# Recurrence of a four-layer graph network: product and sum as one scan, gate biases by matmul

## Chip, cores and metric

One core of a Trainium2 chip runs the whole program. The metric is the device time of one execution in microseconds. Below, PE is the matrix engine TensorE, ACT is ScalarE, DVE is VectorE, POOL is GpSimd and SP is SyncE.

## Reference

The model has four layers, each a graph step and a feed-forward step, over 64 sequences of 128 positions and 128 features, in float32. The change lies in the feed-forward step of the first layer, a recurrence over the 128 positions (B = 64 sequences side by side, H = 128 features on the partitions):

```python
xi = xt @ U_i + b_i
xg = xt @ U_c + b_c
xo = xt @ U_o + b_o
def step(carry, xs):
    h, c = carry
    ...
    i_t = jax.nn.sigmoid(xi_t + h @ V_i)
    g_t = jnp.tanh(xg_t + h @ V_c)
    o_t = jax.nn.sigmoid(xo_t + h @ V_o)
    c_new = h * c + i_t * g_t
    h_new = o_t * jnp.tanh(c_new)
    return ((h_new, c_new), h_new)
```

Step t + 1 needs the h of step t, so the 128 steps can't overlap.

## The kernel before

The program is a row of blocks; between two of them all engines meet at a barrier. The block of the recurrence comes second (lines 385 to 468). It has three programs that run side by side and meet through semaphores, and a POOL part that only clears two tiles at its start (lines 397 and 398).

**PE.** Time is cut into 16 turns of 8 steps (STEPS = 8). A turn uses three of six PSUM banks, one for each gate, and the banks alternate between turns by `par`. For each gate, `inputs` (line 407) writes U times the inputs of a whole turn into its bank in two halves of 256 columns; it is called six times ahead of the first step, and then once in each of the first six steps of a turn for the turn that follows. Each step waits for h (line 412), then adds V times h to its own 64 columns of the three banks, in the order i, c, o (line 417). A float32 matmul is two passes in the trace, each with a weight load, so a step has six passes of 64 columns there. Behind them in PE's order come the `inputs` of the step, in steps 0 to 63 a one-column matmul for row sums that the second layer needs (line 423), and fillers of 256 columns that write a bank that nobody reads (line 425). There are two fillers in a step with `inputs` and three in one without; in steps 0 to 63 there is one fewer.

**ACT.** Each step has three activations from PSUM to the tile `gates`, with the gate's bias (one value on each partition, a column of EXP) as bias operand (line 440): sigmoid for i, tanh for c, sigmoid for o. Then it waits for the cell and takes its tanh (line 443).

**DVE.** Each step has four products or sums of 128 x 64: h times the old cell into `hc` (line 454), gate i times gate c into `ig` (line 458), `hc` plus `ig` into the cell (line 461), and gate o times tanh of the cell, the new h, into `AUX` (line 464). The waits of an instruction are written ahead of it, one to a line. Line 458 has first the wait for gate c (`s.gt`) and then the one for gate i (`s.it`). Line 461 has first the one for `hc`, then the one for `ig`. Line 464 has first the one for gate o, then the one for tanh of the cell.

The biases are loaded by SP in the first block, behind its input transfers, one value on each partition (line 242). EXP is a work tile that holds U, V and biases here; its columns 4096 to 4479 hold weights of the second layer.

## Time and profile before

| | us |
|---|---|
| median of 3 runs | 1961.46 |
| the runs | 1950.76, 1961.46, 1961.59 |
| span of the profiled execution | 1867.1 |
| median less span | 94.4 |
| the steps of the recurrence within the span | from about 115 to 406 |

The profile gives the span of its execution, from the first to the last instruction, and no device time of its own for it; the 94.4 us are what an execution has around that span, if it took as long as the median run. The profile has the busy time of each engine, the start and length of each instruction, what ended an engine's idle time, and the clock that TensorE was granted as a share of its full speed.

### The profile page before, as it was taken

The numbers are of one execution on the slowest core, as the hardware profiler recorded it, in microseconds if no ns is written. First come the engines' busy times: TensorE is split into PE (matmuls) and PEld (weight loads), VectorE is DVE, ScalarE is ACT, GpSimd is POOL, SyncE is SP. The second block draws the span as 40 slices with busy tenths as digits, with TensorE's granted clock in tenths as the row PEclk, the third lists the DMA queues.
The fourth block names the chain that finished last, engine by engine and source line by source line (L and its number), as shares of the span: only waits on it lengthen the run. The fifth ranks groups of instructions, "written<-read, shape, count | busy, mean of one in ns | idle before, by whom it ended". The sixth has DMA issues, their size and how long they took to land. (4 is left out here: it accounts for less than half of the span.)

```text
span 1867.1 us, 43356 instructions
## 1 busy us (share of the span) xinstructions
PE 1627.8 (87%) x13366; PEld 1314.2 (70%) x13366; DVE 1095.9 (59%) x4199; ACT 998.9 (53%) x3116; POOL 786.7 (42%) x1358
## 2 busy tenths in 40 slices
PE   7978899988859987999998888879999888884995
PEld 5756677767759985788887566679999845553542
DVE  7933433348737777699998755523333377763552
ACT  5854444446636656666665433246666534441663
POOL 6710000014426666111111677745565434554675
PEclk9989999999969999899999799989999989995998
DMA  3200000010014420000000511122222253105331
GB/s 114 84 1 1 1 1 1 1 27 1 1 36 134 123 80 1 2 3 2 2 3 3 156 47 48 62 62 70 72 71 72 56 150 86 58 24 88 100 86 35
DMA packets 125926, 91.76 MB, mean 49 GB/s; under 512 B 23591, under 2 KB 116554, under 8 KB 125701
## 3 DMA queue, kind: packets, MB, share of 16 engines
q1 hardware_dynamic: 109110, 61.89, 12.6%
q0 software_dynamic: 13568, 25.90, 4.3%
q10 hardware_dynamic: 3024, 1.21, 0.4%
q8 instruction: 114, 1.87, 0.4%
q14 instruction: 110, 0.90, 0.2%
HBM read 57.71 MB, written 33.30 MB: 49 GB/s over the span
## 5 line engine op out<-in xcount | busy, mean ns | idle before, releaser
L1361 ACT ACTIVATE FEAT<-BANKS,FEAT 128x128 f32<-128x128 f32 x544 | 155.5, 368 | 82.1 <-PE BANKS L1314 82.1
L1206 POOL DMA_INDIRECT scratch_made<-FEAT x136 | 144.9, 1065 | 122.6 <-DVE FEAT L1500 119.8
L1061 ACT ACTIVATE EXP<-BANKS,NEGMAX 128x128 f32<-128x128 f32 x512 | 139.4, 383 | 59.5 <-DVE NEGMAX L1073 59.5
L440 ACT ACTIVATE gates<-BANKS,EXP 128x64 f32<-128x64 f32 x384 | 97.4, 314 | 112.6 <-PE BANKS L417 112.6
L1314 PE MATMUL BANKS<-FEAT 128*128 128x128 f32 x1088 | 145.5, 277 | 0.0
L1323 PE MATMUL BANKS<-AUX,FEAT 128*128 x1088 | 144.5, 276 | 0.4 <-ACT FEAT L1361 0.4
L417 PEld LDWEIGHTS BANKS<-AUX,EXP 128*128 128x128 f32 x768 | 95.4, 191 | 69.7 <-DVE AUX L464 69.6
L1198 POOL DMA_INDIRECT scratch_sent<-FEAT,POS x128 | 125.1, 977 | 38.3 <-issue 37.5
L990 POOL COPY EXP<-AUX 128x32 f32<-128x32 f32 x256 | 42.5, 211 | 217.8 <-PE BANKS L1036 217.8
L1314 PEld LDWEIGHTS BANKS<-FEAT 128*128 128x128 f32 x1088 | 133.9, 194 | 0.0
L1323 PEld LDWEIGHTS BANKS<-AUX,FEAT 128*128 128x128 f32 x1088 | 133.2, 193 | 0.6 <-issue 0.6
L503 POOL TENSOR_SCALAR NEG<-MV 128x4 f32<-128x4 f32 x16 | 3.7, 229 | 303.1 <-DVE MV L176 303.1
L417 PE MATMUL BANKS<-AUX,EXP 128*128 128x64 f32 x768 | 112.8, 283 | 18.6 <-DVE AUX L464 16.6
L425 PE MATMUL BANKS<-FEAT,ident 128*128 128x256 f32 x460 | 126.7, 393 | 0.0
L1500 DVE TENSOR_TENSOR FEAT<-BANKS,B2BC 128x128 f32<-128x128 f32 x136 | 39.5, 290 | 133.1 <-PE BANKS L1323 133.1
L1624 POOL DMA_INDIRECT out_x<-FEAT x96 | 94.1, 980 | 52.1 <-issue 28.4
L846 ACT ACTIVATE WF<-BANKS,BT 128x128 f32<-128x128 f32 x256 | 73.2, 368 | 41.1 <-PE BANKS L820 41.1
L458 DVE TENSOR_TENSOR ig<-gates 128x64 f32<-128x64 f32 x128 | 28.7, 224 | 111.7 <-ACT gates L440 111.7
L1073 DVE TENSOR_REDUCE NEGMAX<-BANKS 128x4 f32<-128x512 f32 x128 | 82.6, 686 | 18.5 <-PE BANKS L1012 18.2
L425 PEld LDWEIGHTS BANKS<-FEAT,ident 128*128 128x128 f32 x460 | 80.8, 191 | 7.4
L1493 DVE COPY FEAT<-AUX 128x512 f32 x136 | 58.1, 427 | 47.1 <-issue 47.0
L1082 DVE SCALAR_TENSOR_TENSOR EXP<-AT,BANKS 128x512 f32<-128x512 f32 x128 | 81.8, 679 | 0.5 <-PE BANKS L1023 0.5
(367 smaller groups left out, 4196.0 us busy)
## 6 DMA issues: line engine op xcount, KB each, us to landing
EXP<-in_L_ffn_W SPq DMA_DIRECT2D x128, 128.0 KB, 2.1
FEAT<-scratch_sent SPq DMA_DIRECT2D x136, 64.5 KB
EXP<-scratch_made SPq DMA_DIRECT2D x32, 256.0 KB, 3.4
FEAT<-scratch_sent SPq DMA_DIRECT2D x96, 65.5 KB, 1.9
X<-in_x SPq DMA_DIRECT2D x16, 256.0 KB, 2.9
STAGE<-in_adj SPq DMA_DIRECT2D x16, 256.0 KB, 3.3
scratch_sent<-NONE SPq DMA_DIRECT2D x48, 65.5 KB, 3.3
scratch_sent<-FEAT,POS POOLq DMA_INDIRECT x192, 2.3
```

The costliest lines, as they stand in the source:

```text
L417: pe.matmul(PS[2 * gate_at + par][:, u * B:(u + 1) * B], wr["V" + gate], cols(HS, j, STEPS * B, u * B, B), start=False, stop=True, skip_gr ...
L425: pe.matmul(PS[7][:, 0:half], ident[:], cols(FEAT, j, STEPS * B, 0, half), start=True, stop=True)
L440: act.activation(gates[:, at, sp_, :], PS[2 * at + par][:, u * B:(u + 1) * B], f, bias=wr["b" + gate]).then_inc(done, 1)
L1061: last = act.activation(tile(EXS[:, par], 4 * k + n), tile(PS[j], c), ACT.Exp, bias=NEGMAX[:, par, 4 * k + n:4 * k + n + 1])
L1073: v.tensor_reduce(NEGMAX[:, par, 4 * k:4 * k + 4].rearrange("p (j c) -> p j c", j=2), BANKS[:, 2 * k:2 * k + 2, 0:NC * T].rearrange("p j ( ...
L1082: v.scalar_tensor_tensor(PTA[:, par, 4 * k * T:4 * (k + 1) * T].rearrange("p (n t) -> p n t", n=4), adj, ADJ_EPS, PS[4 + k].rearrange("p ( ...
L1198: pool.indirect_dma_start(out=sent2, out_offset=bass.IndirectOffsetOnAxis(ap=POS[:, n, b:b + 1], axis=0), in_=OUTBOX[:, i % R_SEND, n, k, ...
L1206: pool.indirect_dma_start(out=made2, out_offset=bass.IndirectOffsetOnAxis(ap=XI_I[:, t % R_IN, H:ROW2], axis=0), in_=YO[:, t % R_OUT, :], ...
L1314: last = pe.matmul(tile(PS[2 + t % 2], c), W1R[:, t % R_W, c * P:(c + 1) * P], XTI[:, t % 3, :], start=True, stop=True)
L1323: last = pe.matmul(PS[4 + t % 2][:, 0:H], tile(HR[:, t % R_H], c), W2_2.rearrange("p c d -> p (c d)")[:, bass.ds(e * F2 + c * H, H)], star ...
L1361: last = act.activation(tile(HR[:, t % R_H], c), tile(PS[2 + t % 2], c), ACT.Gelu, bias=BT[:, c, t:t + 1])
L1624: pool.indirect_dma_start(out=out_rows, out_offset=bass.IndirectOffsetOnAxis(ap=XI3_I[:, t % R3, H + 2:ROW3], axis=0), in_=YO3[:, t % R3, ...
```

## The change

DVE's product `ig` and its sum become one scan. Gate i and gate c are written by ACT into every second element of two tiles of 64 pairs: `by` holds (0, i) and `plus` holds (g, h times c). The scan computes state = by * state + plus along the 128 elements of a partition: at the first element of a pair the state becomes g, at the second i * g + h * c, the new cell. The zeros of `by` are written once by POOL. The scan has three waits ahead of it, in the order `hc`, gate i, gate c.

The activations of the gates lose their bias operand. The biases are loaded as rows of 128 values on partition 0 and added in PSUM by a matmul with one row of contraction: the bias row is the stationary operand, a row of ones, 256 columns wide, the moving one. There is one with each `inputs`, which makes 6 ahead of the first step and 90 within the steps; a step with `inputs` has one filler fewer (1 in steps 64 to 127, 0 in steps 0 to 63).

```diff
--- before.py
+++ after.py
@@ -224,7 +224,7 @@
         wr = {}
         for at, gate in enumerate("cio"):
             wr["U" + gate], wr["V" + gate] = (tile(EXP, 2 * at + k) for k in range(2))
-            wr["b" + gate] = EXP[:, 6 * H + at:6 * H + at + 1]
+            wr["b" + gate] = EXP[0:1, 4608 + at * H:4608 + (at + 1) * H]
         wtop, wbot = EXP[:, 4096:4096 + H], EXP[:, 4096 + H:4096 + 2 * H]
         b1rows = EXP[:, 4096 + 2 * H:4096 + 3 * H]
         with nc.Block() as block:
@@ -239,7 +239,7 @@
                 for gate in "cio":
                     sp.dma_start(wr["U" + gate], a["L0_ffn_U_" + gate]).then_inc(s.later, 16)
                     sp.dma_start(wr["V" + gate], a["L0_ffn_V_" + gate]).then_inc(s.later, 16)
-                    sp.dma_start(wr["b" + gate], column(a["L0_ffn_b_" + gate])).then_inc(s.later, 16)
+                    sp.dma_start(wr["b" + gate], a["L0_ffn_b_" + gate].rearrange("(o h) -> o h", o=1)).then_inc(s.later, 16)
                 sp.dma_start(wtop, a["L1_gnn_weight"][0:H, :]).then_inc(s.later, 16)
                 sp.dma_start(wbot, a["L1_gnn_weight"][H:2 * H, :]).then_inc(s.later, 16)
                 sp.dma_start(b1rows, a["L1_gnn_bias"].partition_broadcast(P)).then_inc(s.later, 16)
@@ -382,12 +382,12 @@
                 unrolled(NG, [(2, hT), (3, back), (2, project), (0, adjacency), (4, xT), (2, conv)])
 
         layer()
-        s = sems("rnn", "zero x_even x_odd g i o gt it ot hc ig c ct h")
+        s = sems("rnn", "zero x_even x_odd g i o gt it ot hc c ct h")
         HS = AUX
-        cell = lb("cell", [P, 2, B])
-        hc = lb("hc", [P, 2, B])
-        ig = lb("ig", [P, 2, B])
-        gates = lb("gates", [P, 3, 2, B])
+        by = lb("by", [P, 2, B, 2])
+        plus = lb("plus", [P, 2, B, 2])
+        made = lb("made", [P, 2, B, 2])
+        gate_o = lb("gate_o", [P, 2, B])
         tanhc = lb("tanhc", [P, 2, B])
         NT = T // STEPS
         ROWSUM = PS[6][:, 0:B]
@@ -395,7 +395,8 @@
             @block.gpsimd
             def _(pool):
                 pool.memset(HS[:, 0:B], 0.0).then_inc(s.zero, 1)
-                pool.memset(cell[:, 1, :], 0.0).then_inc(s.zero, 1)
+                pool.memset(made[:, 1], 0.0).then_inc(s.zero, 1)
+                pool.memset(by[:], 0.0).then_inc(s.zero, 1)
 
             @block.tensor
             def _(pe):
@@ -407,12 +408,15 @@
                     pe.matmul(PS[2 * gate_at + par][:, part * half:(part + 1) * half], wr["U" + gate],
                               cols(FEAT, j, STEPS * B, part * half, half), start=(part == 0), stop=False,
                               skip_group_check=True)
+                    pe.matmul(PS[2 * gate_at + par][:, part * half:(part + 1) * half].rearrange("p (r h) -> p r h", r=2),
+                              wr["b" + gate], ones[0:1, :].unsqueeze(1).to_broadcast([1, 2, half // 2]), start=False, stop=False,
+                              skip_group_check=True)
 
                 def turn(j, par, prefetch):
 
                     for u in range(STEPS):
                         step = j * STEPS + u
-                        pe.wait_ge(s.h if step else s.zero, step if step else 2)
+                        pe.wait_ge(s.h if step else s.zero, step if step else 3)
                         for gate_at, (gate, sem) in enumerate(zip("ico", (s.i, s.g, s.o))):
                             pe.matmul(PS[2 * gate_at + par][:, u * B:(u + 1) * B], wr["V" + gate],
                                       cols(HS, j, STEPS * B, u * B, B), start=False, stop=True,
@@ -421,7 +425,7 @@
                             inputs(j + 1, 1 - par, u // 2, u % 2)
                         if step < B:
                             pe.matmul(ROWSUM[:, step:step + 1], AT[:, step * T:(step + 1) * T], ones[:, 0:1], start=True, stop=True)
-                        for _ in range((2 if prefetch and u < 6 else 3) - (step < B)):
+                        for _ in range((1 if prefetch and u < 6 else 3) - (step < B)):
                             pe.matmul(PS[7][:, 0:half], ident[:], cols(FEAT, j, STEPS * B, 0, half), start=True, stop=True)
                 for gate_at in range(3):
                     for part in range(2):
@@ -434,13 +438,14 @@
                 def turn(j, par):
                     for u in range(STEPS):
                         step, sp_ = j * STEPS + u, u % 2
-                        for at, (gate, made, done, f) in enumerate((("i", s.i, s.it, ACT.Sigmoid), ("c", s.g, s.gt, ACT.Tanh),
-                                                                    ("o", s.o, s.ot, ACT.Sigmoid))):
-                            act.wait_ge(made, step + 1)
-                            act.activation(gates[:, at, sp_, :], PS[2 * at + par][:, u * B:(u + 1) * B], f,
-                                           bias=wr["b" + gate]).then_inc(done, 1)
+                        for at, (gate, ready, done, f, into) in enumerate((
+                                ("i", s.i, s.it, ACT.Sigmoid, by[:, sp_, :, 1]), ("c", s.g, s.gt, ACT.Tanh, plus[:, sp_, :, 0]),
+                                ("o", s.o, s.ot, ACT.Sigmoid, gate_o[:, sp_, :]))):
+                            act.wait_ge(ready, step + 1)
+                            act.activation(into, PS[2 * at + par][:, u * B:(u + 1) * B], f).then_inc(done, 1)
                         act.wait_ge(s.c, step + 1)
-                        act.activation(tanhc[:, sp_, :], cell[:, sp_, :], ACT.Tanh).then_inc(s.ct, 1)
+                        act.activation(tanhc[:, sp_, :], made[:, sp_, :, 1], ACT.Tanh).then_inc(s.ct, 1)
+                act.wait_ge(s.zero, 3)
                 for j in range(NT):
                     turn(j, j % 2)
 
@@ -451,19 +456,18 @@
                         step, q = j * STEPS + u, u % 2
                         if step:
                             v.wait_ge(s.h, step)
-                        v.tensor_tensor(hc[:, q, :], cols(HS, j, STEPS * B, u * B, B), cell[:, 1 - q, :],
+                        v.tensor_tensor(plus[:, q, :, 1], cols(HS, j, STEPS * B, u * B, B), made[:, 1 - q, :, 1],
                                         ALU.mult).then_inc(s.hc, 1)
+                        v.wait_ge(s.hc, step + 1)
+                        v.wait_ge(s.it, step + 1)
                         v.wait_ge(s.gt, step + 1)
-                        v.wait_ge(s.it, step + 1)
-                        v.tensor_tensor(ig[:, q, :], gates[:, 0, q, :], gates[:, 1, q, :], ALU.mult).then_inc(s.ig, 1)
-                        v.wait_ge(s.hc, step + 1)
-                        v.wait_ge(s.ig, step + 1)
-                        v.tensor_tensor(cell[:, q, :], hc[:, q, :], ig[:, q, :], ALU.add).then_inc(s.c, 1)
+                        v.tensor_tensor_scan(made[:, q].rearrange("p b k -> p (b k)"), by[:, q].rearrange("p b k -> p (b k)"),
+                                             plus[:, q].rearrange("p b k -> p (b k)"), 0.0, ALU.mult, ALU.add).then_inc(s.c, 1)
                         v.wait_ge(s.ot, step + 1)
                         v.wait_ge(s.ct, step + 1)
-                        v.tensor_tensor(cols(HS, j, STEPS * B, (u + 1) * B, B), gates[:, 2, q, :], tanhc[:, q, :],
+                        v.tensor_tensor(cols(HS, j, STEPS * B, (u + 1) * B, B), gate_o[:, q, :], tanhc[:, q, :],
                                         ALU.mult).then_inc(s.h, 1)
-                v.wait_ge(s.zero, 2)
+                v.wait_ge(s.zero, 3)
                 for j in range(NT):
                     turn(j, j % 2)
 
```

## Rows read from the trace of the kernel before

**Rows 1.** The page: span, and the chain that ended last, by engine.

```profile
span 1867.1 us, 43356 instructions
...
PE 9%; POOL 4%; issue 3%; ACT 1%; DMA 1%; ACTq 1%; DVE 1%; SPq 0%; POOLq 0%; DVEq 0%
```

**Rows 2.** Busy time by stretch: us, engines, granted clock, DMA share, GB/s.

```profile
110.00:115.30 5.30, 4.57 (x12) 3.74 (x13) 0.22 (x1) 1.28 (x1) 0.24 (x2) 0.54 0.01 3
...
115.30:406.30 291.00, 272.37 (x1538) 211.13 (x1536) 114.73 (x511) 130.19 (x512) 0.00 (x0) 1.00 0.00 1
```

**Rows 3.** Instructions in time, step 38: start us, us, engine, line [idle before <-releaser].

```profile
201.46 0.74 PEld L417 LDWEIGHTS BANKS<-AUX,EXP 128*128 128x128 f32 x6 [0.64 <-DVE AUX L464]
201.46 0.88 PE L417 MATMUL BANKS<-AUX,EXP 128*128 128x64 f32 x6 [0.24 <-DVE AUX L464]
201.93 0.76 ACT L440 ACTIVATE gates<-BANKS,EXP 128x64 f32<-128x64 f32 x3 [0.85 <-PE BANKS L417]
...
202.50 0.22 DVE L458 TENSOR_TENSOR ig<-gates 128x64 f32<-128x64 f32 x1 [0.84 <-ACT gates L440]
202.83 0.23 DVE L461 TENSOR_TENSOR cell<-hc,ig 128x64 f32<-128x64 f32 x1
203.09 0.26 ACT L443 ACTIVATE tanhc<-cell 128x64 f32<-128x64 f32 x1 [0.40 <-DVE cell L461]
203.45 0.22 DVE L464 TENSOR_TENSOR AUX<-gates,tanhc 128x64 f32<-128x64 f32 x1 [0.39 <-ACT tanhc L443]
...
203.72 0.74 PEld L417 LDWEIGHTS BANKS<-AUX,EXP 128*128 128x128 f32 x6 [0.64 <-DVE AUX L464]
```

**Rows 4.** Instructions in time, ACT at 202.25 to 202.30: gate c of that step.

```profile
202.15 0.31 ACT L440 ACTIVATE gates<-BANKS,EXP 128x64 f32<-128x64 f32 x1
```

**Rows 5.** Line 464 by its own view: ns min/median/max, first and last start us.

```profile
L464 DVE TENSOR_TENSOR AUX<-gates,tanhc x128: 224/225/227, 117.3 to 406.1; 128x64 f32<-128x64 f32 x128
```

**Rows 6.** ACT instructions by line and shape: busy us, mean ns | idle before.

```profile
L440 ACT ACTIVATE gates<-BANKS,EXP 128x64 f32<-128x64 f32 x384 | 97.4, 314 | 112.6 <-PE BANKS L417 112.6
...
L443 ACT ACTIVATE tanhc<-cell 128x64 f32<-128x64 f32 x128 | 32.8, 256 | 51.3 <-DVE cell L461 51.3
...
L334 ACT COPY FEAT<-BANKS 128x512 f32<-128x512 f32 x16 | 16.9, 1054 | 2.5 <-PE BANKS L195 2.5
L313 ACT ACTIVATE WB<-BANKS,w_be,w_g 128x512 f32<-128x512 f32 x16 | 12.3, 772 | 0.3 <-PE BANKS L195 0.3
L308 ACT ACTIVATE WD<-BANKS,w_b 128x512 f32<-128x512 f32 x16 | 11.0, 688 | 11.8 <-PE BANKS L368 11.8
...
L330 ACT COPY AT<-BANKS 128x512 f32<-128x512 f32 x16 | 9.4, 588 | 1.5 <-PE BANKS L195 1.5
...
L678 ACT ACTIVATE R<-R,c 64x8 f32<-64x8 f32 x1 | 0.3, 301 | 1.9 <-DVE c L705 1.9
```

**Rows 7.** DVE instructions by line and shape.

```profile
L1088 DVE RECIPROCAL WD<-BANKS 128x128 f32<-128x128 f32 x64 | 60.7, 949 | 0.8 <-PE BANKS L1036 0.8
...
L540 DVE SCALAR_TENSOR_TENSOR X<-WD,X 128x512 f32<-128x512 f32 x16 | 11.1, 693 | 1.6
...
L1925 DVE TENSOR_TENSOR PP<-HOT,RB 128x128 f32<-128x128 f32 x16 | 4.7, 292 | 0.5
```

**Rows 8.** Instructions in time, PE in step 95, which has six long passes.

```profile
331.23 0.88 PE L417 MATMUL BANKS<-AUX,EXP 128*128 128x64 f32 x6
...
331.95 1.51 PE L425 MATMUL BANKS<-FEAT,ident 128*128 128x256 f32 x6
```

**Rows 9.** PE passes by line and shape: one with full rows, one with one row.

```profile
L1036 PE MATMUL BANKS<-EXP 128*32 128x128 f32 x2048 | 69.2, 276 | 0.0
...
L1718 PE MATMUL BANKS<-rbrow,ones 1*128 1x128 f32 x32 | 8.0, 332 | 0.0
```

**Rows 10.** Instructions in time, PE at the start of the block.

```profile
110.73 4.85 PE L407 MATMUL BANKS<-FEAT,EXP 128*128 128x256 f32 x12 [1.98 <-PEq L101]
...
115.42 0.78 PE L417 MATMUL BANKS<-AUX,EXP 128*128 128x64 f32 x6
```

## Prediction

> **What bounds the kernel now.** The page comes first: a span of 1867.1 us, and a chain of work that ended last which reaches over only about a fifth of it and lies near the end [rows 1]. It doesn't say what the recurrence costs, so the stretch is read by itself. By the times of line 464, the 128 steps stand between about 115 and 406 us: from the first product to the last (406.1 - 117.3) / 127 = 2.274 us each [rows 5]. The busy table of that stretch shows PE at 272.4 of 291.0 us with the clock granted at 1.00, ACT at 130.2, DVE at 114.7, and no DMA [rows 2]. PE looks like the bound, but most of that are fillers, and the timeline says otherwise.
>
> The reader is to follow one step there [rows 3, 4]. V's passes begin at 201.46; gate i's activation at 201.93 (0.47 later); gate c's at 202.15 (0.22), which is 314 ns long [rows 6]; the product `ig` at 202.50 and the sum at 202.83, each 0.22 to 0.23; the cell's tanh at 203.09, 256 ns; the new h at 203.45, 224 ns, a length that all three DVE operations share [rows 5]; the next V at 203.72. Every one of these starts right after the one before it ends. The handovers are what is left between end and start: c to `ig` 0.03, `ig` to sum 0.10, sum to tanh 0.04, tanh to h 0.10, h to V 0.05. So a step is a latency chain of 2.26 us over three engines, and whatever shortens a link shortens the kernel 128 times. That the idle time of PE's weight load goes to DVE's line 464 agrees.
>
> One detail matters below: two handovers to DVE take 0.03 or so, and two take 0.10. At `ig` the late wait (gate c) is the first of the two written ahead of the instruction; at the sum and at the new h the late one is the second written. The late wait costs 0.07 more when another stands before it.
>
> **Bias operand gone.** Gate i's start hangs on PE and doesn't move; gate c's hangs on V's pass for c as much as on ACT, and doesn't move either. Its length does. The no-operand tanh of 64 elements takes 256 ns, one with an operand on 8 elements 301 [rows 6]; with the slope between line 440 and line 308, (688 - 314) / (512 - 64) = 0.835 ns for an element, the latter would take 348 at 64, so the operand costs 92 ns. From one operand to two on 512 elements it is 772 - 688 = 84 ns [rows 6]. I take the middle, 0.088 us, so gate c takes 0.226. The bounds are 0 and 0.092. The new output steps over every second element. The only strided output here is line 334's, 1054 ns against line 330's 588 [rows 6], 0.91 ns for an element, or 0.058 us on 64; its step is 256 bytes, the new one 8, so I take 0 and keep 0.058 for the range. The same rows bound the strided reads.
>
> The Trainium skill, in ScalarE: Activation LUTs, section "What ACT_TABLE_LOAD costs", states that each pointer operand adds about 93 ns; by it the sum below would be (0.093 - 0.088) x 128 = 0.6 us better. The trace agrees.
>
> **Product and sum as one scan.** Gate c ends at 202.15 + 0.314 = 202.464 and the tanh begins at 203.09, 0.626 later; of that a handover to the tanh of 0.04 stays. Out go `ig`, the sum and the handover ahead of each: 0.585 us. In come one handover and one scan. The scan's late wait is gate c's, and it now is written third, so it costs 0.10, not 0.03; bounds 0.03 and 0.17. The length of a scan of 128 elements isn't in this trace. The rows give a fixed part and a slope for DVE: line 540 has 693 ns for 512 elements, line 464 has 224 for 64 [rows 5], so 1.05 ns for an element and 157 ns fixed. At one element per slot a scan would take 157 + 128 x 1.05 = 0.291 us, which is what the 128-element product of line 1925 takes, 292 ns [rows 7]. It can't be less. From above, the slowest elementwise row is the reciprocal, 949 ns [rows 7], 6.2 ns for an element. A scan needs the state of the element before, and product and sum stand one behind the other between two states, so I take two slots for an element: 157 + 256 x 1.05 = 0.425 us. That is nearer to the product than to the reciprocal, which works out one value by many operations; a scan has two. Net: 0.585 - 0.102 - 0.425 = 0.058 us, with the handover as it is ahead of the new h (203.45 less 203.09 + 0.256, about 0.10).
>
> The Trainium skill, in DVE: opcode table, instruction layouts, handler registers and perf-mode slots, section "Datapath and trigger behaviour", states that the built-in tensor_tensor_scan feeds back over stages and runs at half throughput. That is the two slots; no row here shows it. At full throughput the sum would be 17 us better on the chain, which is the first rival.
>
> **Bias matmuls and fillers.** A step with `inputs` swaps two filler passes for two one-row passes of the same 256 columns. A one-row pass of 128 columns takes 332 ns, a full-row one 276 [rows 9]; so at worst 0.06 more each. Does PE's row fit the shorter step? In step 95 V begins at 331.23 and six long passes take 1.51 us from 331.95; with 0.38 for the last, they start (1.51 - 0.38) / 5 = 0.23 apart, and the last starts at 333.08 [rows 8]. PE could take the next V at 333.31, 2.08 us after the last. The new chain is 2.26 - 0.146 = 2.12, so PE stays just hidden. If both one-row passes cost 0.06 more, it passes the chain by 0.08 in the 42 such steps from 64 on, 3.4 us; a bound. In steps 0 to 63 four long and two short passes leave far more.
>
> The six bias matmuls ahead of the first step are in nobody's shadow, since V waits behind them in PE's order. The twelve passes there now go from 110.73 to V's at 115.42, 0.39 us each, at a granted clock of 0.54, which is the lower level for most of it, and 1.00 behind it [rows 2, 10]. The twelve added passes come when the clock has risen: 12 x 0.23 = 2.7 us; at the lower level 4.7. POOL's bigger clear ends long before. SP's bias loads are three transfers as before, in the same places of its queue, far ahead of their use; a different number of packets there lies under the first block's last groups. Bias loads, clears and the added DVE waits: 0.
>
> **Sum.** A step saves 0.088 + 0.058 = 0.146 us; 128 x 0.146 = 18.7 us; less 2.7 is 16.0. The span goes from 1867.1 to 1851.1; with the 94.4 us around it unchanged, 1961.5 becomes 1945.5 us. The runs of before themselves lie 11 us apart. About 1%, 19.6 us, is what a measurement can tell from no change.
>
> **Rivals.**
> - *The scan streams one element a slot* (0.291 us). For it: the product's row. Against it: the state. The chain would be 1.98, but PE takes over in the 64 steps with six long passes, at 2.08: 64 x 0.28 + 64 x 0.18 - 2.7 = 27 us gained, 1935. Chance 0.13.
> - *The wait for gate c isn't late*, if it is the scan's own wait and the two others stand ahead. The chain saves 0.07 more, 2.05, below PE's 2.08 in half of the steps: 64 x 0.216 + 64 x 0.18 - 2.7 = 22.6, so 1939. For it: how waits are placed is only read from three pairs. Against: all three fit. Chance 0.10.
> - *The activation gains nothing*, from the stride or because the bias wasn't what cost: 0.058 x 128 - 2.7 = 4.7 gained, 1957. Chance 0.12.
> - *The scan is the new long link* (slower). One instruction takes the place of two, but if its state needs more slots it loses: the break-even is 0.425 + 16.0 / 128 = 0.550 us, or 3.1 ns for an element. At the reciprocal's 949 ns the chain is 2.26 + 0.38, so 128 x 0.378 + 2.7 = 51 us lost, 2012. Against it: only two operations stand in the loop. Chance 0.10.
> - *The clock falls*, because one-row passes drive one row and fillers drove all. Now it is 1.00 throughout [rows 2]. Six long passes at the lower level's 0.39 are 2.3 us, with V's 0.72 more, 3.06, 0.8 us over the chain; each such step loses 3.06 - 2.12 = 0.94, so from 17 of them on (16.0 / 0.94) it ends slower than before. Nothing in the rows shows a fall on one-row work. Chance 0.03.
>
> **Numbers.** The forecast, 1945.5, has 0.52. Leaving out the slow scan and the clock, 1932 to 1959 holds 0.87 less what lies outside by noise, about 0.8: it reaches from the first rival to the third. Faster by over 1% (below 1941.8): the first two rivals and a quarter of the forecast's own spread, 0.36. Slower by over 1%: most of the slow scan and of the clock, 0.07, since a scan between 0.55 and 0.70 us still ends within 1%. Within 1%: 0.57.
>
> **What would show it.** In the changed profile: steps of line 464 2.12 us apart; gate activations at 226 ns; a scan at 425 ns that starts 0.10 behind gate c's end; the busy table at 1.00 clock; V's first pass 2.7 us later. Wrong it goes with a scan far from 425 ns, or with PE busy right up to V in steps 64 to 127: then what ends PE's wait is no longer line 464.

## Result: 124 us slower, and the profile after

| | before | changed |
|---|---|---|
| median, us | 1958.87 (4 runs, 1950.76 to 1961.59) | 2082.57 (4 runs, 2068.05 to 2089.12) |
| span of the profile, us | 1867.1 | 2087.4 |

The ratio is 1.0629, with a 95% interval from 1.0598 to 1.0661: 6.3% slower, where 0.8% faster was forecast.

The page of the changed kernel comes first: its span, PE's busy share and the granted clock, over 40 slices of 52 us.

```profile
span 2087.4 us, 43126 instructions
...
PE   7889999999785998799999677769999788876775
...
PEclk9955555699896998999999788979999999977886
```

The clock is at five tenths in slices 3 to 7 and at six in slice 8; PE is at nine tenths or more in slices 4 to 10. Slices 3 to 8 are the first half of the recurrence. The busy table splits it further (columns as in [rows 2]):

```profile
331.00:402.00 71.00, 71.00 (x213) 51.12 (x213) 15.78 (x54) 16.66 (x71) 0.00 (x0) 0.50 0.00 0
402.00:467.00 65.00, 65.00 (x338) 46.68 (x338) 24.54 (x84) 26.02 (x112) 0.00 (x0) 1.00 0.00 1
```

From 127 to 402 us (the stretches of 68 us ahead of 331 us read alike) the clock is at 0.50, its lower level of 1.2 GHz, and PE is busy for every microsecond of it. In the kernel before, the clock was at 1.00 there and PE had room left [rows 2]. The timeline about 200 us shows what such a step is made of:

```profile
199.77 1.17 PE L408 MATMUL BANKS<-FEAT,EXP 128*128 128x256 f32 x2
...
200.76 0.23 DVE L468 TENSOR_TENSOR AUX<-gate_o,tanhc 128x64 f32<-128x64 f32 x1 [0.39 <-ACT tanhc L447]
...
200.87 1.22 PE L411 MATMUL BANKS<-ones,EXP 1*128 1x256 f32 x2
...
202.46 1.52 PE L421 MATMUL BANKS<-AUX,EXP 128*128 128x64 f32 x6
...
203.77 1.17 PE L408 MATMUL BANKS<-FEAT,EXP 128*128 128x256 f32 x2
```

The `inputs` of two successive steps start at 199.77 and 203.77: a step takes 4.00 us, against 2.27 [rows 5]. The new h is begun at 200.76 and is done at 200.99, but V begins only at 202.46, for PE is still at its own row: `inputs`, the one-row passes of line 411, the one-column passes. The chain isn't the bound any more. The new operations themselves are as forecast. The view of the scan's line and of the activations (ns min/median/max):

```profile
L464 DVE TENSOR_TENSOR_SCAN made<-by,plus x128: 423/425/426, 127.2 to 531.3; 128x128 f32<-128x128 f32 x128
```

```profile
L445 ACT ACTIVATE plus<-BANKS x128: 222/228/231, 126.9 to 530.9; 128x64 f32<-128x64 f32 x128
```

The scan takes 425 ns, the activation without operand 228, strided output and all (314 in [rows 6]).

From 402 us on the clock is back at 1.00. Two steps there:

```profile
450.79 0.74 PEld L421 LDWEIGHTS BANKS<-AUX,EXP 128*128 128x128 f32 x6 [0.29 <-DVE AUX L468]
...
451.45 0.30 PEld L408 LDWEIGHTS BANKS<-FEAT,EXP 128*128 128x128 f32 x2
451.48 0.23 ACT L445 ACTIVATE plus<-BANKS 128x64 f32<-128x64 f32 x1
...
451.84 0.42 DVE L464 TENSOR_TENSOR_SCAN made<-by,plus 128x128 f32<-128x128 f32 x1 [0.85 <-ACT plus L445]
452.09 0.29 PEld L411 LDWEIGHTS BANKS<-ones,EXP 1*128 1x128 f32 x2 [0.33 <-issue]
...
452.71 0.30 PEld L429 LDWEIGHTS BANKS<-FEAT,ident 128*128 128x128 f32 x2 [0.33 <-issue]
...
453.03 0.19 PEld L421 LDWEIGHTS BANKS<-AUX,EXP 128*128 128x128 f32 x1
```

V's weights begin to load at 450.79 and 453.03, 2.24 us apart (the latter still wait for PE), and the median step with `inputs` takes 2.35, against 2.08 for PE in the forecast. The reason stands behind the weight loads: both that of line 411 and the next one of line 429 have 0.33 us of idle time ahead of them, and that of line 408 behind V's has none. From 410 to 530 us 34 of the 68 loads of line 411 are so, one of each pair, and 34 of line 429. PE doesn't load the first one-row weights, nor the first full ones behind them, in the shade of the pass before.

Where the time went, from the starts of the new h (lines 464 and 468) and of the block, against the kernel before as profiled beside the experiments (`e0_before`):

| stretch | before | changed | difference |
|---|---|---|---|
| start of the block to the first new h | 7.5 | 17.7 | +10.2 |
| to that of step 64 | 145.1 | 245.9 | +100.8 |
| to that of step 71 | 16.1 | 30.1 | +14.0 |
| to that of step 127 | 127.7 | 128.0 | +0.4 |

That is 125.4 us, and the medians differ by 123.7: the loss lies in the recurrence. The two spans differ by 140.2; the other 15 us lie in the blocks behind it, where executions of one kernel differ too (the four of the changed kernel are 21 us apart).

One piece of the first row isn't PE's. ACT loads its table of functions once in the block, in 1.28 us. In the kernel before this ran under the `inputs`, at 110.69; in the changed kernel it stands behind the first V:

```profile
110.69 1.28 ACT L440 ACT_TABLE_LOAD   x1 [0.90 <-PEq L101]
```

```profile
125.45 1.28 ACT L445 ACT_TABLE_LOAD   x1 [15.48 <-PE BANKS L421]
```

From V's first pass to the first new h it is 3.37 us here (124.68 to 128.05) against 1.88 before. What is new in ACT's program ahead of the load is its wait for the cleared tiles (`act.wait_ge(s.zero, 3)`). Every kernel below with the scan has that wait and the late load; e1 and e10, which are made from the kernel before, have neither. No run takes the wait out alone.

### The profile page after: what moved, and what is told of

It reads as the page before. It is cut to its first block and busy times, and to the rows that moved or that the text cites. A ratio compares the mean times of both kernels' runs of the same rounds, so it can differ in the third digit from the quotient of the medians.

```text
span 2087.4 us, 43126 instructions
## 1 busy us (share of the span) xinstructions
PE 1804.3 (86%) x13378; PEld 1417.9 (68%) x13378; DVE 1091.9 (52%) x4071; ACT 988.4 (47%) x3116; POOL 789.6 (38%) x1359
## 5 line engine op out<-in xcount | busy, mean ns | idle before, releaser
L464 DVE TENSOR_TENSOR_SCAN made<-by,plus 128x128 f32<-128x128 f32 x128 | 54.4, 425 | 253.3 <-ACT plus L445 253.3
L421 PEld LDWEIGHTS BANKS<-AUX,EXP 128*128 128x128 f32 x768 | 147.8, 270 | 13.4 <-DVE AUX L468 6.8
L421 PE MATMUL BANKS<-AUX,EXP 128*128 128x64 f32 x768 | 151.5, 354 | 0.0
L445 ACT ACTIVATE by<-BANKS 128x64 f32<-128x64 f32 x128 | 29.3, 229 | 224.5 <-PE BANKS L421 224.5
L429 PE MATMUL BANKS<-FEAT,ident 128*128 128x256 f32 x280 | 100.0, 483 | 0.0
L411 PE MATMUL BANKS<-ones,EXP 1*128 1x256 f32 x192 | 98.0, 604 | 0.0
L408 PE MATMUL BANKS<-FEAT,EXP 128*128 128x256 f32 x192 | 93.8, 584 | 2.0 <-PEq L101 2.0
## 6 DMA issues: line engine op xcount, KB each, us to landing
EXP<-in_L_ffn_W SPq DMA_DIRECT2D x128, 128.0 KB, 2.1
```

The lines of the kernel that those rows point to most:

```text
L408: pe.matmul(PS[2 * gate_at + par][:, part * half:(part + 1) * half], wr["U" + gate], cols(FEAT, j, STEPS * B, part * half, half), start=(p ...
L411: pe.matmul(PS[2 * gate_at + par][:, part * half:(part + 1) * half].rearrange("p (r h) -> p r h", r=2), wr["b" + gate], ones[0:1, :].unsqu ...
L421: pe.matmul(PS[2 * gate_at + par][:, u * B:(u + 1) * B], wr["V" + gate], cols(HS, j, STEPS * B, u * B, B), start=False, stop=True, skip_gr ...
L429: pe.matmul(PS[7][:, 0:half], ident[:], cols(FEAT, j, STEPS * B, 0, half), start=True, stop=True)
```

## Experiments

Several kernels have executions that land in two places, 70 to 100 us apart. The profiles show a long one of each such kernel, with the clock lost in the first half of the recurrence, and the mean granted clock on record for each execution goes the same way (0.868 to 0.875 in the long ones of e4, 0.919 to 0.924 in the others). Where that is so, the counts are given. The experiments ran on three chips, on which the kernel before takes between 1866 and 1974 us, so each is compared with the runs of before beside it. The edits of e1 and e10 are against the kernel before, the others against the changed kernel where nothing else is said.

### e0_before: the kernel before, again

> The kernel before, profiled again beside the experiments. The prediction took the 94 us between the span of 1867.1 and the median as time around the span; the changed kernel's profile has 2087.4 us of span in an execution of 2089.1, so only 1.7 lie around it. Then this span is near 1960 to 1975, the recurrence takes the same 291 us with the clock at 1.00, and the 94 us lie in later blocks.

One execution, 1949.4 us with a span of 1947.2. The busy table of the recurrence and of the block from about 1020 us on, here and then in the profile of before:

```profile
110.50:407.40 296.90, 277.33 (x1548) 215.10 (x1548) 114.96 (x512) 131.49 (x513) 0.24 (x2) 0.99 0.00 1
1020.00:1527.00 507.00, 431.65 (x3220) 382.80 (x3220) 207.42 (x951) 239.75 (x793) 291.94 (x306) 0.91 0.22 66
```

```profile
110.20:406.70 296.50, 276.98 (x1548) 214.87 (x1548) 114.99 (x512) 131.47 (x513) 0.24 (x2) 0.99 0.00 1
1024.90:1492.90 468.00, 421.31 (x3218) 377.05 (x3218) 206.93 (x948) 239.90 (x793) 291.76 (x306) 0.94 0.25 72
```

The recurrence is the same to 0.4 us, at the same clock. The later block isn't: 507 against 468, and the last block, from there to the end, adds as much again (1947.2 - 1527 against 1867.1 - 1493, 420 against 374). The 94 us of the prediction weren't around the span; the profile of before comes from an execution that was that much shorter in those blocks, at a higher granted clock there (0.94 against 0.91 in the first of them). On the chip of the last experiments the kernel before took 1865.7, so a difference of this size goes with the chip; on which chip the profile of before was taken is not on record. The difference forecast for the recurrence isn't touched by it.

### e1_one_row: one filler becomes a one-row pass, without the scan

```diff
     inputs(...):
         pe.matmul(PS[2 * gate_at + par]..., wr["U" + gate], ...)
+        pe.matmul(PS[7][:, 0:half]..., wr["U" + gate][0:1, :],
+                  ones[0:1, :]...to_broadcast([1, 2, half // 2]), start=True, stop=True)
...
-    for _ in range((2 if prefetch and u < 6 else 3) - (step < B)):
+    for _ in range((1 if prefetch and u < 6 else 3) - (step < B)):
```

> The kernel before with one thing changed: in each step with inputs one filler (two passes of 128 rows) becomes two one-row passes of the same 256 columns into the bank nobody reads, and six such matmuls stand ahead of the first step. Bias operand, product and sum stay. Theory R (one-row passes don't count for the clock as full-row passes do): the granted clock stays at the lower level from the start of the block to about step 64, steps there take about 4.0 us instead of 2.27, some 115 to 125 us slower than before. Theory C (columns are what counts; the low clock of the changed kernel comes from its shorter chain or from the scan): the clock rises at the first step as before, steps of 2.27, only the start is longer, 3 to 5 us slower.

2099.2 us, ratio 1.0618 (1.0579 to 1.0657). Its busy table:

```profile
127.00:250.00 123.00, 123.00 (x385) 89.16 (x384) 28.57 (x128) 38.44 (x128) 0.00 (x0) 0.50 0.00 1
250.00:253.00 3.00, 3.00 (x17) 1.96 (x17) 1.02 (x5) 1.02 (x4) 0.00 (x0) 1.00 0.00 0
253.00:400.00 147.00, 147.00 (x451) 106.08 (x452) 33.43 (x150) 45.07 (x150) 0.00 (x0) 0.50 0.00 1
```

With the bias operands, product and sum of before, this swap, with the six one-row matmuls that it puts ahead of the first step, makes the whole loss: 125 us. The low stretch ends at 400 us as in the changed kernel, with 3 us of the upper level in between: the clock was up in the middle of the stretch, and such steps didn't keep it. Theory C falls: neither the scan nor a shorter chain is needed.

### e10_less_filler: one filler fewer, no one-row pass

```diff
-    for _ in range((2 if prefetch and u < 6 else 3) - (step < B)):
+    for _ in range((1 if prefetch and u < 6 else 3) - (step < B)):
```

> The kernel before with one filler fewer in each step with inputs, and no one-row pass anywhere: the full-row work of a step is that of the changed kernel. If one-row passes are nothing to the clock and the missing full-row work is the cause, the clock falls within steps 0 to 63 as it does with them, though the start of the block, whose passes all have full rows, lifts it first; PE then has less to do, so a step takes 2.6 to 3.0 us at the lower level, 20 to 45 us slower than before. If the one-row passes themselves keep the clock down, it holds at 1.00, steps of 2.27, same as before.

1909.5 us against 1865.7 beside it, ratio 1.0231 (1.0206 to 1.0256), 44 us slower. Its busy table, and a step:

```profile
118.00:200.00 82.00, 79.03 (x304) 71.24 (x304) 26.43 (x118) 34.20 (x116) 0.00 (x0) 0.55 0.00 1
200.00:280.00 80.00, 78.87 (x294) 71.06 (x294) 24.75 (x110) 33.07 (x111) 0.00 (x0) 0.52 0.00 1
...
330.00:420.00 90.00, 75.87 (x411) 57.80 (x410) 35.09 (x156) 39.87 (x157) 0.00 (x0) 0.98 0.00 1
```

```profile
201.44 2.05 PE L425 MATMUL BANKS<-FEAT,ident 128*128 128x256 f32 x4
...
202.16 0.23 DVE L464 TENSOR_TENSOR AUX<-gates,tanhc 128x64 f32<-128x64 f32 x1 [0.39 <-ACT tanhc L443]
...
202.86 0.34 PEld L417 LDWEIGHTS BANKS<-AUX,EXP 128*128 128x128 f32 x1
```

PE's fillers, from 201.44 to 203.49, hold up the next V, whose weights load at 202.86 although h was ready at 202.39. The clock rises at 116 us, falls at 122.5 without any one-row pass, and is at 0.52 to 0.55 from 118 to 280; it comes back for 3 us each at 140 and at 232 and isn't kept. So taking the filler away is enough. PE has less to do, and steps with `inputs` take 2.73 us in the low stretch by the starts of line 464, not 4.00. What the one-row passes add is time of PE's own at that level, by the difference of these steps 1.28 us in each. They don't make up for the fillers they displace.

### e2_full_rows: the bias matmuls on 128 rows

```diff
-    wr["b" + gate] = EXP[0:1, 4608 + at * H:4608 + (at + 1) * H]
+    wr["b" + gate] = EXP[:, 4608 + at * H:4608 + (at + 1) * H]
...
-    sp.dma_start(wr["b" + gate], a["L0_ffn_b_" + gate].rearrange("(o h) -> o h", o=1))
+    sp.dma_start(wr["b" + gate], a["L0_ffn_b_" + gate].partition_broadcast(P))
...
-    wr["b" + gate], ones[0:1, :].unsqueeze(1).to_broadcast([1, 2, half // 2])
+    wr["b" + gate], shares[:].unsqueeze(1).to_broadcast([P, 2, half // 2])   # 1/128 everywhere
```

> The changed kernel with the bias matmuls on all 128 rows: the stationary operand is the bias row repeated on 128 partitions, the moving one holds 1/128 everywhere. Same passes, same columns. Theory R: the clock rises at the start of the block, steps take 2.12 us and the kernel ends where the prediction had it, 16 us faster than before (about 1943 to 1946). Theory C: nothing changes against the changed kernel, about 2080. Repeated values could load the array less than mixed ones do; then it ends between the two.

Four executions: 1961.9, and 2041.6 to 2050.6, with 1974.4 for before beside them. The profile is of one of the three long ones:

```profile
114.00:121.00 7.00, 5.53 (x29) 4.84 (x28) 0.65 (x3) 2.00 (x5) 0.00 (x0) 0.97 0.00 0
121.00:340.00 219.00, 218.99 (x771) 195.88 (x771) 56.27 (x193) 59.92 (x256) 0.00 (x0) 0.50 0.00 1
```

Neither theory has this. The clock rises at the start, as R has it, and falls at 121 us, though PE's long passes all have full rows again and are as many as before. (That the rows of the bias operand are all alike isn't needed for it: e4, without them, falls in the same way.) It comes back at 340, in steps that take 3.41 us till then, not 4.00. Behind it steps take 2.16 us, and the 2.35 of the changed kernel are gone: those were the one-row passes' own price. The one execution that was short is 12 us faster than before.

### e3_no_bias and e4_scan_only: the two halves on DVE and ACT

In both the bias matmuls are out and the fillers those of before; e4 has the bias operand again, and e3 leaves the biases of the recurrence out.

```diff
-    pe.matmul(... wr["b" + gate], ones[0:1, :]... start=False, stop=False, ...)     # e3 and e4
-    for _ in range((1 if prefetch and u < 6 else 3) - (step < B)):
+    for _ in range((2 if prefetch and u < 6 else 3) - (step < B)):
...
-    act.activation(into, PS[2 * at + par][:, u * B:(u + 1) * B], f)
+    act.activation(into, PS[2 * at + par][:, u * B:(u + 1) * B], f, bias=wr["b" + gate])   # e4
```

> The changed kernel without its bias matmuls and with the fillers of before (the biases of the recurrence are left out of the computation). Scan and activations without operand stay. Both theories but C: clock at 1.00 from step 0, steps of 2.12 us, 128 x 0.146 = 18.7 us faster than before. Theory C: if the shorter chain or the scan keeps the clock low, steps near 4 us and about 2080.

> The kernel before with the scan alone: bias operand and fillers as before, outputs of gates i and c at every second element. By the prediction's terms a step saves 0.058 us, 7.4 us in all. If strided outputs cost on ACT, less; a rival that the wait for gate c is not late gives 16 us.

e3: 1959.8 us, ratio 0.9936 (0.9905 to 0.9967), eight executions of eight with the clock up (a mean of 0.915 to 0.921). Its recurrence:

```profile
110.30:393.70 283.40, 272.34 (x1548) 214.90 (x1548) 112.26 (x384) 120.01 (x513) 0.54 (x3) 0.99 0.00 1
```

That is 13 us less than 296.5, with steps of 2.155 where 2.12 was forecast. The rest is in the rows of the changed kernel above: gate c starts at 451.48 and takes 0.228, so it ends at 451.71, and the scan starts at 451.84. The handover is 0.13, not 0.10; the two waits that stand behind the first share one semaphore instruction, which takes 50 ns where one with a single wait takes 21.

e4: six executions from 1969.4 to 1976.1, ratio 0.9986 (0.9963 to 1.0010), and five from 2042.6 to 2047.5. The scan alone gains nothing that could be measured; by its steps of 2.247 it is 0.02 a step, where 0.058 was forecast and the handover took 0.033 of it. The five lose the clock at 121 us and have it back at 336:

```profile
121.00:336.00 215.00, 215.00 (x756) 192.17 (x756) 55.22 (x189) 76.22 (x252) 0.00 (x0) 0.50 0.00 1
```

PE's passes are exactly those of before, and its steps are 0.02 us shorter, not longer. Yet the kernel before kept the clock in all of its 31 executions beside the experiments (a mean of 0.913 or more). What does differ on PE is the first step, where V of the second waits behind ACT's late table load:

```profile
115.18 1.28 ACT L442 ACT_TABLE_LOAD   x1 [5.82 <-PE BANKS L418]
...
118.24 0.88 PE L418 MATMUL BANKS<-AUX,EXP 128*128 128x64 f32 x6 [1.56 <-DVE AUX L466]
```

PE is idle for 1.56 us there, against 0.25 in the kernel before, and the clock falls 2.5 us later, at 120.8. The profile of e2 has 1.48 us of idle time and the fall 0.2 behind it. But e3 has 1.38 and kept the clock. So this idle time goes with the falls that the kernel before never has, and doesn't decide them alone; no run has the scan with the table load early.

### e5_warm_start and e6_filler_back: is it the start, or the steps?

```diff
     for gate_at in range(3):
         for part in range(2):
             inputs(0, 0, gate_at, part)
+    for _ in range(12):                                                   # e5
+        pe.matmul(PS[7][:, 0:half], ident[:], cols(FEAT, 0, STEPS * B, 0, half), start=True, stop=True)
...
-    for _ in range((1 if prefetch and u < 6 else 3) - (step < B)):
+    for _ in range((1 + (step < B) if prefetch and u < 6 else 3) - (step < B)):      # e6
```

> The changed kernel with twelve more fillers (24 full-row passes) between the six bias matmuls and the first step, some 7 us. Theory S (what keeps the clock low is only the start, where half of the passes have one row; a clock that is up stays up): steps 0 to 63 go at 2.16 us, and the kernel lands about 120 us below the changed one, near 1960. Theory R (the steps themselves have too little full-row work: V, the two passes of inputs and the one-column passes): the clock rises ahead of step 0 and falls again within the first steps; 7 us slower than the changed kernel, or the same.

> The changed kernel with its dropped filler back in steps 0 to 63 alone: the full-row work of a step there is that of before, the one-row passes come on top. Theory R: the clock comes up early in the recurrence, if the start lets it, and steps 0 to 63 take about 2.35 us, PE-bound as the steps from 64 on are now; about 105 us faster than the changed kernel. If the start alone decides, the clock stays low, each step gets 0.85 us longer than now, and it is some 40 us slower than the changed kernel.

e5: 2088.4 us, ratio 1.0654 (1.0617 to 1.0691):

```profile
128.00:135.00 7.00, 5.91 (x31) 4.77 (x29) 0.88 (x3) 2.00 (x5) 0.00 (x0) 0.97 0.00 0
135.00:408.00 273.00, 273.00 (x842) 196.73 (x841) 61.25 (x210) 65.84 (x280) 0.00 (x0) 0.50 0.00 1
```

The clock is up as the first step begins, and gone again 7 us later. So a low clock at the start isn't needed for the loss. That the steps can't hold it isn't shown by this run alone: the fall, at 134.6, comes right behind 1.09 us in which PE waits for the first new h, with the table load ahead of it. The 3 us of e1 at 250 do: PE was busy in all of them, and the clock was lost.

e6: five executions from 2082.5 to 2126.7, median 2103.4; the ratio 1.0638 (1.0600 to 1.0675) is that of the three shortest. The profile is of one of 2114.2. PE's row at 200 us:

```profile
199.96 1.20 PE L429 MATMUL BANKS<-FEAT,ident 128*128 128x256 f32 x2
200.96 1.38 PE L421 MATMUL BANKS<-AUX,EXP 128*128 128x64 f32 x6
...
204.82 1.20 PE L429 MATMUL BANKS<-FEAT,ident 128*128 128x256 f32 x2
```

```profile
110.00:414.00 304.00, 303.81 (x896) 218.82 (x896) 56.68 (x194) 62.12 (x261) 0.54 (x3) 0.50 0.00 0
```

Theory R misses: the clock doesn't come up early. The case of the start alone has its step right, 0.85 us longer (4.86 from one filler to the next, against 4.01), and its 40 us in the profile, where the new h of step 64 starts at 414 and not at 374. But e5 had shown that the start alone isn't it either. The full-row work of a step is back to that of before, and with the clock down from the start and PE the bound the step only gets longer. Why it doesn't lift the clock is argued, not shown: in a step of 4.86 us the same full-row work is thinner than in one of 2.27.

### e7_reworked, e8_spread, e9_later: the gain without the loss

e7 keeps the bias operand for gates i and o, whose ends nobody waits for last, and takes gate c's bias by full rows in the two steps of a turn without `inputs`, in a filler's place. It writes the late wait first, ahead of the scan and of the new h. From step 64 on one filler has half the columns.

```diff
-    v.wait_ge(s.hc, step + 1)
-    v.wait_ge(s.it, step + 1)
     v.wait_ge(s.gt, step + 1)
+    v.wait_ge(s.hc, step + 1)
+    v.wait_ge(s.it, step + 1)
     v.tensor_tensor_scan(...)
-    v.wait_ge(s.ot, step + 1)
     v.wait_ge(s.ct, step + 1)
+    v.wait_ge(s.ot, step + 1)
...
+    if prefetch and u >= 6:
+        bias_c(1 - par, u - 6)          # 128 rows, as in e2
...
+    wide = half // 2 if step >= B and fill == 0 else half
```

> A version meant to keep the scan's gain without the loss: gates i and o keep their bias operand (they aren't late), gate c alone gets its bias by a matmul with 128 rows in the two steps of a turn without inputs, in the place of a filler; the late wait is written first ahead of the scan and of the new h; from step 64 on one filler has half its columns. By the terms measured so far: 2.155 us less 0.10 at the scan and 0.07 at the new h gives steps of 1.99 us if the clock holds, 128 x 0.28 = 36 us less than before. If one-column passes and thinner fillers let the clock fall in steps 0 to 63, those take 3.4 us each and it is 40 us slower than before.

Four executions: 1918.7, and 2014.3 to 2019.1, beside 1961.7 for before. The short one is 43 us below before, where 36 was forecast. The profile is of a long one:

```profile
120.00:335.00 215.00, 215.00 (x758) 192.32 (x757) 55.50 (x191) 69.20 (x252) 0.00 (x0) 0.50 0.00 1
335.00:461.00 126.00, 125.27 (x758) 98.95 (x756) 55.02 (x188) 64.32 (x252) 0.00 (x0) 1.00 0.00 1
```

With the clock up a step takes 1.99 us. With it down it takes the 3.41 us of e2 and e4.

e8 and e9 differ from e7 in where the one-column sums stand and in how full the early steps are. In e8 all steps of the first half are fuller; in e9 only the first eight are, and the others have what they had in e7. The edit is against e7:

```diff
-    if step < B:                        # sum number step
+    if step % 2 == 0:                   # e8: sum number step // 2
+    if 8 <= step < B + 8:               # e9: sum number step - 8
...
-    for fill in range((2 if prefetch else 3) - (step < B)):
-        wide = half // 2 if step >= B and fill == 0 else half
+    for fill in range(2 if prefetch else 3):                         # e8
+        wide = half // 2 if fill == 0 else half
```

> The reworked version with the one-column sums for the second layer spread over all 128 steps, one in every second, and a filler of half the columns added to the steps up to 63, so each step has V, four long and two half passes of full rows, as its steps from 64 on have. Those held the clock in every run. Expected: 1.00 throughout, steps of 1.99 us, 36 us less than before, and no run that lands 55 us higher. If the falls come from the block's start and not from thin steps, some runs still fall, but come back within a few steps.

> The reworked version with the one-column sums in steps 8 to 71 in place of 0 to 63, so only the first eight steps have the denser work. All falls seen so far came within the first three steps. If the start decides, the clock holds in every run, 1.99 us a step, 36 us less than before; if thin steps let it fall at any time, it falls behind step 8 in some runs, and they land 55 us higher.

e8: 1833.3 us against 1865.7 for before beside it, ratio 0.9818 (0.9798 to 0.9838), four executions within 5 us. e9: 1835.3, ratio 0.9823 (0.9800 to 0.9846), four within 7 us. That is 32 and 30 us less than before, where 36 was forecast. The recurrence of e8, and a step of it:

```profile
110.00:373.00 263.00, 260.09 (x1681) 219.91 (x1681) 112.21 (x385) 131.84 (x513) 0.68 (x4) 0.99 0.00 1
```

```profile
200.60 0.23 DVE L480 TENSOR_TENSOR AUX<-gate_o,tanhc 128x64 f32<-128x64 f32 x1 [0.33 <-ACT tanhc L459]
...
201.57 0.23 ACT L456 ACTIVATE plus<-BANKS 128x64 f32<-128x64 f32 x1
...
201.84 0.42 DVE L476 TENSOR_TENSOR_SCAN made<-by,plus 128x128 f32<-128x128 f32 x1 [0.75 <-ACT plus L456]
```

Gate c begins at 201.57 and, at 228 ns, ends at 201.80; the scan begins at 201.84, 0.04 later. The tanh, 257 ns from 200.31, ends at 200.57, and the new h begins at 200.60. The order of the waits is worth 0.10 at the scan and 0.07 at the new h. Both versions are faster than the kernel before by their whole intervals. e9 says more than e8: its profile has the clock at 1.00 from 116 to 370 us, with steps 8 to 63 as thin as in e7. Its forecast had this for the case that the start of the recurrence decides.

## Why the prediction was wrong, point by point

**"The clock falls", chance 0.03.** This rival came true, and it is the step that failed: the sum took the clock of 1.00 as given with the fillers swapped. It was 0.50 for 275 us, with steps of 4.00 us where 2.12 was forecast, and 125 us were lost where 16 were to be gained. The prediction looked at the clock of before, found 1.00 throughout, and took the margin for large; "nothing in the rows shows a fall" was true, and no evidence. e10 shows that one filler fewer in a step loses the clock; e1 that one-row passes in its place don't save it. The fillers were counted as work that hides or is hidden, and not as what holds the clock. The rival's reason, one row against all, was half of it: in e10 no one-row pass is left and the clock falls too.

**The price of the fall.** Put at 3.06 us for a step with six long passes; measured were 4.00 (e1 and the changed kernel) for steps with four long ones, two of them one-row, which the prediction gave no price. The prediction had V's passes at 0.72 at either level; they take 1.31 at the lower one (from V at 202.46 to `inputs` at 203.77 above), and a one-row pair costs 1.28 (e1 less e10) where a long pair was put at 0.78. That it is slower from some 17 such steps on was right in kind; it lasted for 71.

**One-row passes at most 0.06 dearer each.** Wrong by the row it was read from. The length of a pass in [rows 9] isn't its price; the idle time ahead of its weight load belongs to it, and a sign of that stood in the same profile of before:

```profile
L1718 PEld LDWEIGHTS BANKS<-rbrow,ones 1*128 1x128 f32 x32 | 4.9, 190 | 9.7 <-issue 9.3
```

32 loads of one row had 9.7 us of idle time ahead of them. It is a sign and no price: 12 of them had 0.76 and 16 none, and 192 other one-row loads (line 1789) had 5.3 us in all. In the changed kernel it is 0.33 ahead of the one-row load and 0.33 ahead of the full one behind it. With the clock up, a step with `inputs` takes 2.35 us from step 71 on, 0.20 over the 2.155 of e2 and e3, where "0.08 as a bound" was given. This alone would have taken away the gain of the second half.

**The start, 2.7 us.** It was 10.2 with the first step. The clock had risen by 114.8 us before, and here it didn't. The upper bound of 4.7 had the pass of before at the lower level and not the one-row pass. And 1.5 us of it lie behind V's first pass, most of them the table load: "Bias loads, clears and the added DVE waits: 0" leaves out the wait that ACT got, and from V's first pass to the first new h e3, at the full clock, takes 3.01 where 1.88 was.

**Scan 0.425, activation 0.226.** Right: 425 ns and 228. The two slots for an element are measured now, and the stride of 8 bytes costs nothing. The Trainium skill, in DVE: opcode table, instruction layouts, handler registers and perf-mode slots, section "Datapath and trigger behaviour", has the built-in tensor_tensor_scan at half throughput; the 425 ns agree.

**Handover 0.10 for the scan.** Nearly: 0.13, within its bounds of 0.03 and 0.17. That is why e3 gains 13 to 15 us and not 18.7. The rule read from three pairs of waits holds; e8 shows it by turning the order round.

**The 94 us around the span.** Wrong, and without effect on the forecast difference: 1.7 to 2.2 us lie around a span (2087.4 in 2089.1, 1947.2 in 1949.4). A median that lies 5% above the profile's span had to be read as another execution, not as overhead.

## What to carry to other kernels

Where fillers stand beside a latency chain, they are part of the design: before one is dropped or replaced, ask what PE does in that step that loads the whole array, and treat "clock 1.00" as one side of a switch whose distance isn't shown. Where the clock fell and PE became the bound at the lower level, it came back for good only as the steps changed; what held it, in all eight executions of e8 and e9, was denser steps at the start. Look too at what idles PE in the first step, as the late table load did here. A bias on a gate that isn't the last one costs nothing as an operand, so only the late one is worth moving; and the semaphore that comes last should be the wait written first, worth 0.07 to 0.10 us a step here.

## What the runs showed of the hardware

PE was busy for all of 275 us and the clock stayed at its lower level. The Trainium skill, in TensorE: Matmul & The Clock Gate, section "What's actually happening", has it that a block of the chip watches how busy PE has been, and that activity releases the throttle. The busy share of the profile, whose ends of passes are modelled, doesn't foretell this: it was 1.00 here at the lower level, and 0.94 in the kernel before at the upper one (272.4 of 291.0 us). In e1 one-row passes filled PE's time where fillers had stood, and the clock was down for all but some 3 of the 273 us from 127 to 400.

A clock lost early stays lost long: e2, e4 and e7 fell at 120 or 121 us, in the first three steps, and came back only as the steps from 64 on began, at 335 to 340.

One thing stays open. The kernel before, e3 and e4 have the same passes on PE in the steps; e3 kept the clock in eight executions of eight, with steps 0.09 us shorter than e4's, and the kernel before in all, with steps 0.02 longer; e4 kept it in six of eleven. So how thin the steps are doesn't explain it alone. e4 has the idle time behind the late table load, and the kernel before doesn't; but e3 has it too (1.38 us), as have e8 (1.06) and e9 (1.28), all with the clock kept, and e7 (1.29), which lost it. e2 and e7 kept the clock in one execution of four each. e8 and e9 kept it in four of four each, by denser first steps, but on one chip and with no run of e7 beside them. Two rivals are untested: the chip, and the table load moved ahead of the first V. What decides it in a single execution wasn't found.
